# Strassen's seven products for the down projection of ten more rounds, with w_down going through DRAM in both passes

## What is computed

```python
x = layernorm(x + attention(x, wq, wk, wv, wo))         # 32 query heads, 8 key/value heads of 32, RoPE, causal
gate = x_flat @ (gate_t * gate_s[:, None]).T            # x_flat: 2048 x 1024; gate_t, up_t: 3584 x 1024, int32 in -1..1
up = x_flat @ (up_t * up_s[:, None]).T
out = (silu(gate) * up) @ (down_t * down_s[:, None]).T  # down_t: 1024 x 3584, int32 in -1..1
x = layernorm(x + out)
```

## Time and profile before

| | us |
|---|---|
| median of 3 runs (lowest, highest) | 1866.36 (1864.86, 1866.38) |
| the profiled execution | 1864.6 |
| its span, first to last instruction | 1862.9 |

### The profile page before, as it was taken

One profiled execution on the slowest core, in us unless ns is written; L12 is line 12 of the kernel. 1 busy time (PEld: TensorE's weight loads), 2 busy tenths in 40 slices (PEclk: granted clock), 3 DMA queues, 4 the chain that ended last, 5 costly groups with the idle time before them and its releaser, 6 DMA issues.

```text
span 1862.9 us, 27050 instructions
## 1 busy us (share of the span) xinstructions
PE 1808.5 (97%) x10384; PEld 875.0 (47%) x10384; DVE 1187.1 (64%) x2059; ACT 709.8 (38%) x1112; POOL 529.4 (28%) x806
## 2 busy tenths in 40 slices
PE   7989999999999998999999999999999999999998
PEld 4545555555555543444444444444444444444444
DVE  7877768678767763446544444755656765667646
ACT  5343444444434444436433343342232322222221
POOL 1354546455445554231000000211321211122103
PEclk9999999999999998999999999999999999999999
DMA  8443234334324397557654353649411121222301
GB/s 256 110 109 74 54 86 132 75 78 114 98 46 114 81 217 200 215 199 269 244 176 151 108 194 116 221 150 205 137 61 59 67 78 42 80 100 81 117 12 79
DMA packets 228304, 233.10 MB, mean 125 GB/s; under 512 B 183888, under 2 KB 184144, under 8 KB 228176
## 3 DMA queue, kind: packets, MB, share of 16 engines
q1 hardware_dynamic: 227312, 230.99, 41.8%
q10 hardware_dynamic: 864, 0.39, 0.2%
HBM read 122.55 MB, written 72.88 MB: 105 GB/s over the span
## 4 chain that ended last, share of the span: by engine, by line
PE 87%; DVE 6%; issue 2%; SPq 2%; DMA 1%; POOL 1%; ACT 1%; DVEq 0%; ACTq 0%; POOLq 0%
PE bank L1068 32%; PE bank L964 20%; PE bank L1088 13%; PE bank L1101 6%; PE bank L1013 4%; PE bank L976 3%; PE bank L1000 3%; PE bank L1028 2%; PE bank L979 1%; DVE down_forms L1425 1%; SPq L1623 1%; DVE gate_blocks L1419 1%; DVE row_max L1285 0%; DVE up_blocks L1409 0%; DVE down_forms L1402 0%
## 5 line engine op out<-in xcount | busy, mean ns | idle before, releaser
L1068 PE MATMUL bank<-x_forms,weight_forms 128*128 128x512 f16 x3136 | 700.4, 379 | 11.1 <-DVE up_blocks L1409 3.7
L1068 PEld LDWEIGHTS bank<-x_forms,weight_forms 128*128 128x128 f16 x3136 | 305.3, 98 | 385.1 <-DVE gate_blocks L1409 7.1
L1155 ACT ACTIVATE p_tiles<-bank 128x512 f32<-128x512 f32 (+1 forms) x352 | 192.9, 557 | 295.8 <-PE bank L1000 292.7
L1285 DVE TENSOR_REDUCE row_max<-bank 128x1 f32<-128x384 f32 (+3 forms) x352 | 220.2, 636 | 97.5 <-PE bank L979 96.6
L1088 PE MATMUL bank<-down_forms 128*128 128x512 f16 (+1 forms) x1168 | 259.6, 378 | 2.4 <-issue 2.4
L964 PE MATMUL bank<-wq_parts,xT_parts 128*128 128x256 f16 x1536 | 216.9, 274 | 9.2 <-DVE wq_parts L1249 8.9
L1444 DVE TENSOR_TENSOR acc<-bank,acc 128x512 f32<-128x512 f32 x188 | 127.7, 687 | 123.5 <-PE bank L1088 64.4
L1482 POOL TENSOR_SCALAR_AFFINE_SELECT p_tiles<-p_tiles 128x128 f32<-128x128 f32 (+2 forms) x352 | 138.4, 400 | 220.7 <-ACT p_tiles L1155 219.8
L1088 PEld LDWEIGHTS bank<-down_forms 128*128 128x128 f16 x1168 | 114.6, 98 | 138.4 <-issue 4.9
L964 PE MATMUL bank<-wo_parts,att_parts 128*128 128x512 f16 x672 | 171.7, 384 | 2.1 <-DMA att_parts<-att_spill 2.1
L964 PEld LDWEIGHTS bank<-wq_parts,xT_parts 128*128 128x128 f16 x1536 | 144.8, 98 | 61.0 <-issue 13.2
(11 more groups left out here) (117 smaller groups left out, 1977.2 us busy)
## 6 DMA issues: line engine op xcount, KB each, us to landing
weight_forms_spill<-weight_forms SPq DMA_DIRECT2D x28, 896.0 KB, 5.5
weight_forms<-weight_forms_spill SPq DMA_DIRECT2D x28, 896.0 KB, 4.5
x_forms_spill<-x_parts SPq DMA_DIRECT2D x56, 256.0 KB, 2.4
w_page<-gateT SPq DMA_DIRECT2D x28, 512.0 KB, 5.0
w_page<-upT SPq DMA_DIRECT2D x28, 512.0 KB, 3.8
w_page<-downT SPq DMA_DIRECT2D x28, 512.0 KB, 4.2
att_spill<-att_made SPq DMA_DIRECT2D x64, 128.0 KB, 2.2
down_forms<-x_spill SPq DMA_DIRECT2D x16, 512.0 KB, 3.5
```

Source lines behind the costliest of these rows:

```text
L1068: t = nc.tensor.matmul(strassen[bank_set(use)][to][:, :], w_form[:, use % 4, A_FORMS[a_form], k * P:(k + 1) * P], xF[:, :, B_FORMS[b_form] ...
L1155: nc.scalar.activation(p32[j][:, h0:h0 + heads, :], bank[5 + m % 2][:, 0:heads * n].rearrange("p (h c) -> p h c", c=n), ACT.Exp, scale=SCO ...
L1285: nc.vector.tensor_reduce(mx[:, u % 2, i, h0:h0 + ROW_HEADS[i]], bank[3 + m % 2][:, 0:ROW_HEADS[i] * n].rearrange("p (h c) -> p h c", c=n) ...
```

## The change

The rounds 0 to 9 of pass 1 make their down products by Strassen's seven products as well, as pass 2 does. The last group (rounds 10 to 13) stays plain in both passes. So that the forms can be made in the ring buffers, w_down takes one way in both passes: its pages are cast in place (float16 into the first half of the page buffer), each page is stored to DRAM from there (28 stores of 256 KB in place of 14 of 512 KB), and every round of both passes loads its two pages from DRAM (`d_in`: 28 loads in place of 14). The cast of w_down then waits for no room and no end of the projections, but the load of the page after the next waits for the store of a w_down page to land. The first down product waits until all of `hidden` of round 1 is made, and in pass 1 the loads of `ds` and `x1_row` wait for the group of rounds 6-7, as they do in pass 2.

```diff
-DOWNS = [(q, m) for q in range(PASSES * ND) for m in range(PAIRS * NPR if ND <= q < PASSES * ND - 1 else 2 * PT)]
+DOWNS = [(q, m) for q in range(PASSES * ND) for m in range(PAIRS * NPR if q % ND < ND - 1 else 2 * PT)]
...
 def plain(n):
 
-    return n < NF or n % NF >= PLAIN
+    return n % NF >= PLAIN
...
     p, r = divmod(n, NF)
-    if p == 0:
-        return DOWN_OF[r - 4] if r > 3 else None
-    return DOWN_OF[p * NF + min(r - 3, PLAIN - 1)] if r > 2 else p * ND - 1
+    if r > 2:
+        return DOWN_OF[p * NF + min(r - 3, PLAIN - 1)]
+    return p * ND - 1 if p else None
...
-            for _ in range(4 if n < NF else 10):
+            for _ in range(10):
                 if left and DOWN_ROUNDS[left[0][0]][-1] < n:
                     down_at[left.pop(0)] = clock
-                    clock += one if n < NF else one / 2
+                    clock += one / 2
...
         put(PE, at + 5, one * len(rounds) / (2 if plain(rounds[0]) else 4), "down", q, m, after=after + (
-            [("down", *DOWNS[d - 1])] if d else [("att_scale", NU - 1, UG - 1)]) + ([("acc", *DOWNS[d - 2])] if d > 1 else []))
+            [("down", *DOWNS[d - 1])] if d else [("att_scale", NU - 1, UG - 1), ("hidden", 1, 3)]) + ([("acc", *DOWNS[d - 2])] if d > 1 else []))
...
-        if w == 2:
-            room = outputs + ([("down", *DOWN_LAST[DOWN_OF[r - 4]]), ("d_store", r - 4)] if r > 3 else [])
...
-        if w == 2 and c == 1:
-            put(SY, at + 6, .4, "d_store", r, moves=PAGE_MOVES, after=[("w_cast", w, r, 0), ("w_cast", w, r, 1)])
-    for n in range(NF, ROUNDS):
-        for use in range(2 * n, 2 * n + 2):
+        if w == 2:
+            put(SY, at + 1, .4, "d_store", w, r, c, moves=PAGE_MOVES / 2, after=[("w_cast", w, r, c)])
+    for n in range(ROUNDS):
+        for use in range(2 * n, 2 * n + 2) if n >= NF else ():
...
         def place_of(n):
 
-            return n % 4 if n < NF else (1, 2, 0, 3)[n % NF - PLAIN]
+            return (1, 2, 0, 3)[n % NF - PLAIN]
...
                     on.wait_ge(s_scale_att, 4 * NU * UG)
+                    on.wait_ge(s_hid, 8)
...
                     else:
-                        projections_over(on)
-                        place_free(on, r)
-                        on.wait_ge(s_dst[r % 4], 16 * (r // 4))
-                        to = wd_p[place_of(r)][:, c, :]
+                        to = w_page[n % 2][:, 0:D // 2].bitcast(F16)
...
                     on.wait_ge(s_cast, n - 1)
+                    if n > 1 and w_order[n - 2][0] == 2:
+                        on.wait_ge(s_dst[n % 2], 16 * (w_order[n - 2][1] + 1))
...
                 elif kind == "d_store":
-                    n = which[0]
-                    for c in range(2):
-                        on.wait_ge(s_cast, cast_n["w_cast", 2, n, c])
-                    e.dma_start(wd_dram[n], wd_p[place_of(n)].rearrange("p c d -> p (c d)")).then_inc(s_dst[n % 4], 16)
+                    n, (_, r, c) = w_n[which], which
+                    on.wait_ge(s_cast, n + 1)
+                    e.dma_start(wd_dram[r, :, c * D:(c + 1) * D], w_page[n % 2][:, 0:D // 2].bitcast(F16)).then_inc(s_dst[n % 2], 16)
...
                     place_free(on, n)
-                    for i in range(4):
-                        on.wait_ge(s_dst[i], 16 * len(range(i, NF, 4)))
+                    if n:
+                        projections_over(on)
+                    else:
+                        attention_over(on)
+                    for i in range(2):
+                        on.wait_ge(s_dst[i], 16 * (min(n, NF - 1) + 1))
                     to = wd_p[place_of(n)].rearrange("p c d -> p (c d)") if plain(n) else wd_f[n % NF % 3][:, 0:4, :].rearrange("p f c -> p (f c)")
-                    e.dma_start(to, wd_dram[n - NF]).then_inc(s_din[(n - NF) % 4], 16)
+                    e.dma_start(to, wd_dram[n % NF]).then_inc(s_din[n % 4], 16)
...
                 elif kind == "ds_load":
                     outputs_over(on)
-                    if which[0]:
-                        on.wait_ge(s_down, DOWN_N[DOWN_LAST[which[0] * ND + ND - 3]] + 1)
+                    on.wait_ge(s_down, DOWN_N[DOWN_LAST[which[0] * ND + ND - 3]] + 1)
```

More of the change, by code:

```diff
@@ L576, in ffn_plan @@
             after = [("hid_lo", rounds[-1], HID_PLAIN[-1])]
-            after += [("w_cast", 2, r, c) for r in rounds for c in range(2)] if p == 0 else [("d_in", r) for r in rounds]
+            after += [("d_in", r) for r in rounds]
         put(PE, at + 5, one * len(rounds) / (2 if plain(rounds[0]) else 4), "down", q, m, after=after + (
-            [("down", *DOWNS[d - 1])] if d else [("att_scale", NU - 1, UG - 1)]) + ([("acc", *DOWNS[d - 2])] if d > 1 else []))
+            [("down", *DOWNS[d - 1])] if d else [("att_scale", NU - 1, UG - 1), ("hidden", 1, 3)]) + ([("acc", *DOWNS[d - 2])] if d > 1 else []))
         room = [("acc", *DOWNS[d - 1])] if d else []
@@ L589, in ffn_plan @@
             put(PO, at + one + 1, 2.4, "scale_row", tile, after=[("acc", q, m), ("ds_scale", p)])
-            put(SY, at + one, .4, "last_x1", tile, moves=PAGE_MOVES, after=over + ([("down", *DOWN_LAST[q - 1])] if p else []) + (
+            put(SY, at + one, .4, "last_x1", tile, moves=PAGE_MOVES, after=over + [("down", *DOWN_LAST[q - 1])] + (
                 [("add_x1", tile - 1)] if tile else []))
@@ L597, in ffn_plan @@
         at = down_at[p * ND + ND - 2, 0]
-        put(SY, at, .4, "ds_load", p, moves=PAGE_MOVES, after=over + ([("down", *DOWN_LAST[p * ND + ND - 3]), ("acc", *DOWN_LAST[p * ND - 1])] if p else []))
+        put(SY, at, .4, "ds_load", p, moves=PAGE_MOVES, after=over + [("down", *DOWN_LAST[p * ND + ND - 3])] + (
+            [("acc", *DOWN_LAST[p * ND - 1])] if p else []))
         put(VE, at + 4, 1.3, "ds_scale", p, after=[("ds_load", p), ("bound", 1)])
@@ L606, in ffn_plan @@
         at = (use_at[use] - 12 if w < 2 else use_at[2 * r + 1] - 12 + c) if r else start
-        put(SY, at - 6, .4, "w_load", w, r, c, moves=PAGE_MOVES, after=scores + ([("w_cast", *pages[i - 2])] if i > 1 else []))
+        put(SY, at - 6, .4, "w_load", w, r, c, moves=PAGE_MOVES, after=scores + ([("d_store" if pages[i - 2][0] == 2 else "w_cast", *pages[i - 2])] if i > 1 else []) + (
+            [("w_load", *pages[i - 1])] if i else []))
         room = []
@@ L625, in ffn_plan @@
         at, old = use_at[2 * n + 1] - 6, room_after(n)
-        put(SY, at, .4, "d_in", n, moves=PAGE_MOVES, after=[("d_store", n - NF), ("down", *DOWN_LAST[old])] + (
-            [("acc", *DOWN_LAST[old])] if old == ND - 1 else []))
+        put(SY, at, .4, "d_in", n, moves=PAGE_MOVES, after=[("d_store", 2, n % NF, 0), ("d_store", 2, n % NF, 1)] + (
+            [("down", *DOWN_LAST[old])] if old is not None else outputs) + ([("acc", *DOWN_LAST[old])] if old == ND - 1 else []))
         if not plain(n):
@@ L1081, in tensor_program @@
                         for r, c in itertools.product(rounds, range(2)):
[L1082 to L1085, removed]
+                            on.wait_ge(s_din[r % 4], 16 * din_n(r))
                             k = BLOCKS.index((c, i % 2))
@@ L1663, in sync_program @@
                     outputs_over(on)
[L1664 to L1665 removed]
+                    on.wait_ge(s_down, DOWN_N[DOWN_LAST[tile // PT * ND + ND - 3]] + 1)
                     e.dma_start(x1_row, x1_dram[tile]).then_inc(s_xrow, 16)
```

8 lines of the change are left out of this document (4 added, 4 removed).

## The result

The changed kernel takes 1885.87 us (median of 4 runs, 1884.71 to 1890.98) where the kernel before, in the same session, takes 1865.61: ratio 1.0115, 95% interval 1.0095 to 1.0135. The forecast was 1856.2, faster; the time lies far outside the range of 1849 to 1866. The profiled execution took 1884.7 us, 20.1 more than that of before.

A forecast was written before the change was run, and what follows sets the result against it. PE, busy 1808.5 of 1862.9 us, was taken as the bound. Matmuls -17.3, start wait -2.6, Strassen waits +6.7 and first group +3.0 sum to -10.2 us off the median 1866.36: 1856.2 us, range 1849 to 1866.

The forecast's parts named there:

- the 80 matmuls: Ten rounds of pass 1 go from 64 down matmuls to 56, 80 fewer at 0.216 us: 17.3 us saved.
- the way of w_down: Start of pass 1: the cast no longer waits behind the output projection, 2.6 us gained; added stores and loads cost nothing.
- VectorE's work in a middle group: Pass 1: VectorE's share in a middle group rises from 35.88 of 75.97 to 53.6 of 72.6 us.
- I take those of pass 2 as they stand: Strassen rounds in pass 1 bring the same PE waits as in pass 2: 6.7 us, bounds 2 and 13.4.
- 3 us for the first group: First group of pass 1: PE stands 3 us at its down products and round 3's chain, bounds 0 and 9.
- The prediction's own sign of being wrong: Over 10 us of PE waits in pass 1 would make the forecast wrong.
- The new wait for hidden of round 1: Pass 1: this wait comes as late as pass 2 bears or long before it matters, so it costs nothing.
- round 3's chain behind the first group: One high part, three low parts, a copy and a sum: some 4 us, of which PE covers 2.6.
- Which changes nothing: VectorE operations lengthened beside GpSimd, 0.432 to 0.474 us: 3.4 us of VectorE on 80 forms of weights, no effect.
- rival C: VectorE's hand-over of the two down banks becomes the bound: at 0.2 us each, 28 us lost, 1874.5 us; chance 0.09.
- Nothing is later for it: Loading w_down into a ring buffer waits for the group with the round three before, as hidden does: no cost.

The follow-up runs named there:

- pages only: Changed kernel with w_down through its pages and DRAM in both passes, but plain down products and four places in pass 1: 1862.93 us, 0.9986 to the kernel before.
- VectorE's forms: Changed kernel with the four forms of hidden made by VectorE in place of GpSimd, both passes: 1864.29 us; with rounds 0 to 3 plain as well, 1848.68 us.

## Why the prediction was wrong

**Right:** the 80 matmuls; that the way of w_down hides its stores and loads and gains 2.6 us (pages only, 0.9986); VectorE's work in a middle group (53.6 us forecast, 54.95 measured); that pass 2 stays as it is.

**"I take those of pass 2 as they stand", 6.7 us, and 3 us for the first group.** This is the step that failed. 9.7 us of losses in pass 1 were forecast; 40 us were measured. The prediction's own sign of being wrong, over 10 us of PE waits in pass 1, is there with 31.7 us. By parts, from the kernels above (each is a difference of medians, good to 2 or 3 us):

- The changed kernel stands 22.9 us above pages only, and saves 17.3 us of matmuls: 40.2 us lost by ten Strassen rounds in pass 1.
- GpSimd's forms in pass 1: 21.6 - 8.6 = 13.0 us.
- Rounds 0 to 3, with VectorE's forms: from 1864.29 to 1848.68 us, and 32 matmuls (6.9 us) more on top: 22.5 us. The first group has 11.6 of them, where 3 us were forecast and 9 was the upper bound; the second group has 10.9, and nothing was set aside for it beyond its share of the 6.7 us. The trace with VectorE's forms shows most of it up to 950 us: PE waits 4.14 us for a row of the output projection's sum (line 1330), 5.42 for the sum at 884 us, 3.17 for the load of w_down and 1.5 in three short waits, 14.2 us, and the half clock behind them cost 4.0. The rest is not located.
- The last six rounds, with VectorE's forms: 10.4 - 7.4 = 3.0 us. That leaves 1.7 us, within what medians of different sessions leave open.

Where GpSimd made the forms, a middle group lost 0.23 and 1.75 us in place of the 0.36 that pass 2 shows. My reading, which no run separates: pass 2 hides the same stretched operations in the time that pass 1 fills with forms of weights. A wait taken from a less busy place is a lower bound, not a price.

Two terms put at nothing or too low belong to the same step. The new wait for hidden of round 1 was costed at nothing: at 851.64 us PE waits 2.06 us for it and then has half its clock, and ahead of it four forms of w_down take VectorE 3.82 us in place of 1.8. And round 3's chain behind the first group, "some 4 us", is 4.8 with low parts at the 0.951 us used elsewhere in the prediction.

**"Which changes nothing."** I compared two means, 0.432 and 0.474 us, and called the effect a tenth. But most of the forty operations of that row don't meet GpSimd at all. The kernel before had it (shortest, median and longest, ns):

```profile
L1402 DVE TENSOR_TENSOR down_forms<-down_forms x40: 411/425/1112, 1335.9 to 1669.7; 128x512 f16<-128x512 f16 x40
L1425 DVE TENSOR_TENSOR down_forms<-up_blocks,down_forms x40: 673/685/1756, 1350.9 to 1680.9; 128x512 f16<-128x512 f32 x40
```

Those that meet GpSimd take two and a half times as long (1.11 us for 0.42, and in the row of the low parts 1.75 for 0.68). By the means and these lengths, an estimate, they are three in forty of the forms and ten in forty of the low parts, and where I followed them they stand in the chain, since GpSimd works when a round's forms are due. What the Trainium skill, "SBUF — State Buffer", section "SBUF: two separate sides", says, that one of the two blocks for the whole instruction, is what the timeline shows: where GpSimd multiplies acc by the scale, 2.5 us each, two VectorE operations of 0.69 us take 4.95 us.

```profile
1200.56 5.10 POOL L1507 TENSOR_TENSOR acc<-acc,down_forms 128x1024 f32<-128x1024 f32 x2 [12.82 <-DVE acc L1440]
...
1201.26 4.95 DVE L1421 TENSOR_TENSOR down_forms<-gate_blocks,down_forms 128x512 f16<-128x512 f32 x2
```

I had the rule, put it aside by a mean, and gave rival C 0.09. C's place was wrong too: the hand-over of the down banks cost PE 3.4 us in pass 1 (1.77 and 1.67); the sums of gate and up, and through them the products, were late.

**"Nothing is later for it"**, of the load of w_down into the ring buffer. It starts when the buffer is free (936.86 us) and takes some 3.5 us, while hidden is written at once: at 940 us PE waits 3.10 us for that load and 0.82 for the form made from it.

**The clock** was no term of the sum. It cost some 8 us at the start; these are inside the parts above, not beside them.

## What to carry to other kernels

A mean over all instances of an operation doesn't price the instance on the critical chain: look up the one that stands beside the other engine, in the timeline, before an engine's added work is called cheap. An operation given to GpSimd saved nothing here, where VectorE reads two operands from SBUF meanwhile: VectorE does the same work in the same busy time, and sooner. Work that trades matmuls for work of other engines belongs where those engines have room: with VectorE's forms, four rounds at the start of pass 1 save 6.9 us of matmuls and lose 22.5 us, and the six behind them save 10.4 and lose 3.0.

## What had not been expected of the hardware

Idling in the middle of a busy stretch cost PE more than the idle time: after waits of 2.06 to 4.76 us its granted clock was at 0.50 for 3.4 to 6.9 us, and 67 useless matmuls in five of the waits made the kernel 8.3 us faster. At 1021 and 1239 us waits of 1.75 and 2.01 us were not followed by it, nor was that of 2.68 us in pass 2. The length of the wait alone doesn't decide: behind the same wait in pass 2 (2.69 us) the trace of pages only has a clock of 0.58 for 3.4 us, and behind the 2.44 us ahead of the last group the kernel before has 0.56 and the changed one 1.00. What decides it these runs don't tell. It also moves a single execution by some 1.5 us.
